# Two running sums for the first expert stage, picks made in the routers, and earlier loads of up-weights

## The chip, the cores and the metric

One core of a Trainium2 chip runs the whole program. The time is device microseconds from start to end of one execution.

## The reference

The input is 4 x 1024 tokens of 256 features. The program is two layers; what the change touches is the mixture-of-experts block, which both have at their end:

```python
h = gelu(concat([xf, stats(xf)]) @ r1_w.T + r1_b)
probs = softmax(h @ r2_w.T)                       # 32 experts
topp, topi = top_k(probs, 2)
score = where(routed, probs, -inf)
idx = argsort(-score, axis=0)[:cap].T             # cap = 160 tokens for each expert
gate, upv = split(xf[idx] @ w_up.T, 2)            # per expert, 256 -> 2 x 512
ye = (silu(gate) * upv) @ w_down.T                # 512 -> 256
out = zeros.at[idx].add(w * ye)                   # each token is in at most two experts
```

An adapter for each pair of experts is added in the same way. Layer 0 is: x + 0.5 ffn(layernorm x), a causal attention over sums of keys, x + 0.5 ffn again, and then x + moe(layernorm x). Layer 1 is a linear attention (relu of keys and queries, `kv = k.T v` for each of the four sequences, output `q kv / (q sum k)`), added to x, and the moe block again.

## The kernel before

**Stages.** The program runs in stages with a barrier of all engines between them: the first feed-forward, attention (to 602 us), the first router `ffn_router` (to 723 us), the first `dispatch` (to 1157 us), the linear attention with the second router in it, `linear_router` (to 1405 us), and the second `dispatch` (to the end). Rows of the input lie in 32 tiles of 128 tokens, four tiles to a group; a batch is one sequence, two groups. Every engine has its own instruction list, written out by hand in a function of each stage (`sync` for SP's DMA queue, `gpsimd` for POOL, `tensor` for PE, `scalar` for ACT, `vector` for DVE); they meet in semaphores only. `Chain.link` makes DVE wait for its own last operation.

**Routers.** `RouterFront` normalizes each group, makes statistics of a row, and brings the logits of 32 experts for each token into `m.prob`; `take` on ACT is its last step. `ffn_router` has the feed-forward around it. Its first step is `layernorm_var` on DVE for all 32 tiles, the power -0.5 on POOL (`rstd_of`, line 112), and `shift` on DVE (line 1890); then ACT normalizes group by group.

**Dispatch** is `route` and then `experts`, in one block. In `route` DVE finds for each token its two best experts (`pick1`, `pick2`, lines 2055 to 2068), the sum of exponentials, and scores; then `Choice` searches, over 15 rounds, the score from which an expert's 160 tokens are taken, for the first 16 experts at once (`counts`, `decide`; `beside(k)` puts other DVE work into round k), makes lists of tokens, and POOL gathers the first rows. The second half's search runs beside the first experts. `values` on POOL runs beside the first rounds. Up to line 2073 these are operations over 32 tiles x 32 experts, 1024 values in each of 128 partitions.

**Experts** are done in quads of four, eight quads; a turn is two quads. PE's order, of one expert: five products up (the last is the adapter's), the down products of the expert before, and so on; weights lie in four buffers, and SP loads the next expert's after the down product that used the buffer has ended (`turn` in `sync`, `load_expert`), the adapters with every second expert:

```python
sp.wait_ge(full[u_down[n].bank], down[n])
m.load_expert(sp, t * 2 * EQ + n + EQ, n % EQ)     # 1 MB w_up, 0.5 MB w_down
if n % 2:
    m.load_adapter(sp, t * EQ + n // 2 + EQ // 2, n % EQ // 2)
```

A quad's 4 x 160 results are five tiles: one of 128 for each expert, and the four tails of 32 in the fifth. ACT weighs them into `y` (line 2370), and POOL adds them to the rows of x in DRAM (`add`, line 2237, an indirect DMA that adds). Within one such DMA, or between two that are under way together, no row may come twice. A token may be in two experts of a quad, but then once as its first choice and once as its second; so each quad is added in two phases of five tiles, the first choices and, once these have landed, the second. A next quad waits for both. Only in the last quad two tiles go whole, one after the other (`ALONE`): each has one expert's tokens.

**Linear stage.** SP loads x back from the sum (`x_sum`), eight groups of 512 KB, with 1.2 MB of weights behind the second. DVE makes statistics of a batch (`stats`, line 87), `norm` writes the normalized rows, PE turns them, makes keys and values tile by tile (`kv`), and sums their products; for each tile DVE writes `k_row` (line 2636), for which the sum waits. DVE's `stats(b + 2)` stands at a batch's end, ahead of the next batch's first `k_row`.

## Time and profile before

| | |
|---|---|
| median of 3 runs | 1841.35 us (1838.83 to 1843.05) |
| the profiled execution | 1842.41 us, its span 1840.7 us |
| busy: PE, DVE, ACT, POOL | 1513.0, 957.9, 728.7, 561.4 us |
| mean granted clock of PE | 0.901 of full speed |
| moved by DMA | 212.10 MB, mean 115 GB/s |

Times in the rows are microseconds from the span's start. PE is busy for 82% of the span, but not evenly: in both dispatches there is a stretch before the experts in which it waits for the search, and one behind them in which only POOL's adds run.

### The profile page before, as it was taken

What the parts mean: (1) busy time and instruction counts of PE and PEld (TensorE: products, weight loads), DVE (VectorE), ACT (ScalarE), POOL (GpSimd) and SP (SyncE); (2) the same over time, 40 slices, a digit from 0 to 9 for tenths busy, and PEclk for the clock granted to TensorE, in tenths of its full rate; (3) what the DMA queues carried; (4) which work ended last, traced back from release to release, by engine and by line L of the source; (5) the groups of instructions that cost most, each with busy time, mean ns of one, the idle gap of its engine ahead of it and who ended that gap; (6) DMA issues with size and microseconds to landing.
All of it is one profiled execution on the core that took longest, in us unless ns stands there. A gap on an engine that the chain in (4) does not pass through costs nothing. (4 is left out here: it accounts for less than half of the span.)

```text
span 1840.7 us, 26894 instructions
## 1 busy us (share of the span) xinstructions
PE 1513.0 (82%) x9512; PEld 1155.9 (63%) x9512; DVE 957.9 (52%) x2637; ACT 728.7 (40%) x1773; POOL 561.4 (30%) x465
## 2 busy tenths in 40 slices
PE   6899989999998595549999996589983559998994
PEld 5556544555554463439889896355552549888994
DVE  8766677888773495754521111366555754421120
ACT  4222157666665484415323232123332425322331
POOL 6422300000001441231637345222101231545445
PEclk9989989999999797559999998799995569999997
DMA  3033462333200133125869785411014026789774
GB/s 101 27 124 117 123 116 54 77 58 75 51 25 2 35 110 139 54 43 168 237 205 240 222 224 86 125 39 42 24 60 175 6 46 203 215 234 245 226 213 46
DMA packets 113492, 212.10 MB, mean 115 GB/s; under 512 B 20085, under 2 KB 79386, under 8 KB 104154
## 3 DMA queue, kind: packets, MB, share of 16 engines
q1 hardware_dynamic: 87066, 178.93, 30.6%
q0 software_dynamic: 26304, 31.60, 11.4%
q8 instruction: 69, 1.13, 0.3%
q14 instruction: 53, 0.43, 0.1%
HBM read 158.71 MB, written 51.38 MB: 114 GB/s over the span
## 5 line engine op out<-in xcount | busy, mean ns | idle before, releaser
L952 DVE TENSOR_REDUCE attnm_top<-psum 128x1 f32<-128x384 f32 (+3 forms) x384 | 212.8, 597 | 56.4 <-PE psum L1037 52.3
L1174 ACT ACTIVATE attnm_prob<-psum 128x512 f32<-128x512 f32 (+1 forms) x384 | 192.1, 530 | 88.3 <-PE psum L1047 81.6
L2237 POOL DMA_INDIRECT out<-moe2e_y,moe_scatter_i x76 | 119.2, 1568 | 146.6 <-ACT moe2e_y L2370 77.7
L2292 PE MATMUL psum<-moe1e_xgT,moe_w_up 128*128 128x160 f32 x1024 | 154.7, 307 | 8.6 <-issue 6.1
L2292 PE MATMUL psum<-moe2e_xgT,moe_w_up 128*128 128x160 f32 x1024 | 153.6, 305 | 9.6 <-issue 7.2
L2415 DVE SCALAR_TENSOR_TENSOR moe2e_h<-moe2e_gate,psum 128x160 f32<-128x160 f32 x160 | 50.4, 320 | 212.6 <-ACT moe2e_gate L2344 212.4
L2415 DVE SCALAR_TENSOR_TENSOR moe1e_h<-moe1e_gate,psum 128x160 f32<-128x160 f32 x160 | 50.6, 321 | 212.2 <-ACT moe1e_gate L2344 212.0
L2237 POOL DMA_INDIRECT x_sum<-moe1e_y,moe_scatter_i x76 | 119.4, 1571 | 136.6 <-ACT moe1e_y L2370 80.3
L2292 PEld LDWEIGHTS psum<-moe1e_xgT,moe_w_up 128*128 128x128 f32 x1024 | 145.9, 195 | 11.8 <-issue 11.8
L2292 PEld LDWEIGHTS psum<-moe2e_xgT,moe_w_up 128*128 128x128 f32 x1024 | 145.0, 194 | 12.7 <-issue 12.7
L1344 POOL DMA_INDIRECT moe_xg<-xn_rows,moe_gather_i x80 | 83.6, 1045 | 163.6 <-DVE moe_gather_i L1528 101.9
L938 POOL TENSOR_TENSOR attnm_tail_v<-attnm_v_tail,attnm_tail_p 128x256 f32<-128x256 f32 x32 | 19.8, 620 | 343.5 <-PE psum L1089 284.5
L1035 PE MATMUL psum<-attn_mask_ts,ident_bf 128*128 128x128 bf16 x512 | 105.9, 226 | 9.6 <-DVE attnm_top L952 7.6
L1037 PE MATMUL psum<-attnm_k_hat,attnm_q_hat 96*128 96x512 bf16 (+3 forms) x384 | 106.9, 306 | 0.0
L1047 PE MATMUL psum<-attnm_q_hat,attnm_k_hat 99*128 99x512 bf16 (+1 forms) x288 | 98.4, 345 | 1.4 <-ACT attnm_prob L1174 0.6
L2344 ACT ACTIVATE moe1e_gate<-psum 128x160 f32<-128x160 f32 x160 | 47.4, 301 | 112.1 <-PE psum L2292 111.8
L2344 ACT ACTIVATE moe2e_gate<-psum 128x160 f32<-128x160 f32 x160 | 47.2, 300 | 112.5 <-PE psum L2292 112.2
L2304 PE MATMUL psum<-moe2e_h,moe_w_down 128*128 128x160 f32 x512 | 80.4, 300 | 2.0 <-ACT moe2e_yT L2352 2.0
L2304 PE MATMUL psum<-moe1e_h,moe_w_down 128*128 128x160 f32 x512 | 80.4, 300 | 2.0 <-ACT moe1e_yT L2352 2.0
L1035 PEld LDWEIGHTS psum<-attn_mask_ts,ident_bf 128*128 128x128 bf16 x512 | 50.5, 100 | 48.3 <-issue 24.3
L1060 PE MATMUL psum<-attnm_prob,attn_v_aug 128*32 128x512 f32 (+1 forms) x768 | 78.7, 527 | 0.0
L2304 PEld LDWEIGHTS psum<-moe2e_h,moe_w_down 128*128 128x128 f32 x512 | 72.9, 190 | 2.8 <-ACT moe2e_yT L2352 2.8
(426 smaller groups left out, 3234.6 us busy)
## 6 DMA issues: line engine op xcount, KB each, us to landing
moe_w_up<-in_expert_up SPq DMA_DIRECT2D x64, 1024.0 KB, 5.5
moe_w_down<-in_expert_down SPq DMA_DIRECT2D x64, 512.0 KB, 7.2
attnm_q_hat<-q_parts SPq DMA_DIRECT2D x72, 128.0 KB, 4.6
moe_a_up<-in_adapter_up SPq DMA_DIRECT2D x32, 256.0 KB, 6.6
q_parts<-attnf_q_part SPq DMA_DIRECT2D x12, 512.0 KB, 2.8
attnm_k_hat<-k_parts SPq DMA_DIRECT2D x72, 64.0 KB, 2.3
x_res<-in_x SPq DMA_DIRECT2D x8, 512.0 KB, 8.7
v_tails<-attnf_v_tail SPq DMA_DIRECT2D x4, 1024.0 KB, 4.3
```

The source lines that it names most:

```text
L952: nc.vector.tensor_reduce(top[:, n // QUADS % 2, tiles[0]:tiles[-1] + 1, hh:hh + 1], s.ps[:, u.bank, 0:len(tiles) * width].rearrange("p (t ...
L1035: nc.tensor.matmul(out[:, width - P:width], s.identb[:], o.mask_ts[:, tile % 2, :], start=(i == 0), stop=False, skip_group_check=True)
L1037: ins = nc.tensor.matmul(out, q_hat[r][0:MROW, h, tile * P:(tile + 1) * P], k_hat[r][0:MROW, h, 0:width], start=False, stop=True, skip_gro ...
L1047: nc.tensor.matmul(s.ps[:, u.bank, at:GROUP], k_hat[r][0:MROW + NPART, h, j * P:(j + 1) * P], q_hat[r][0:MROW + NPART, h, g * GROUP + at:( ...
L1060: ins = nc.tensor.matmul(s.ps[32 * h:32 * h + 32, u.bank, at:GROUP], o.v_aug[:, first:first + 32], prob[:, i % NPROB, at:GROUP], start=(j ...
L1174: nc.scalar.activation(prob[:, i % NPROB, at:GROUP], s.ps[:, u.bank, at:GROUP], ACT.Exp).then_inc(taken[u.bank], 1)
L1344: pool.indirect_dma_start(self.xg[:, q, k, :], None, self.rows, bass.IndirectOffsetOnAxis(ap=self.gather_i[:, at:at + 1], axis=0), bounds_ ...
L2237: nc.gpsimd.indirect_dma_start(total, bass.IndirectOffsetOnAxis(ap=rows, axis=0), y[:, q, k, :], None, bounds_check=TOKENS + SPARE - 1, oo ...
L2292: ins = nc.tensor.matmul(s.ps[:, u.bank, half * CAP:(half + 1) * CAP], lhsT, xgT[:, q, c, k * CAP:(k + 1) * CAP], start=(c == 0), stop=(c ...
L2304: ins = nc.tensor.matmul(s.ps[:, u.bank, o * CAP:(o + 1) * CAP], lhsT, h[:, n % 2, i, :], start=(i == 0), stop=(i == PAIRS - 1))
L2344: nc.scalar.activation(gate[:, i, :], s.ps[:, u.bank, 0:CAP], ACT.Silu).then_inc(silu, 1)
L2415: nc.vector.scalar_tensor_tensor(out=h[:, n % 2, i, :], in0=gate[:, i, :], scalar=1.0 if i < INTER // P else SCALE_A, in1=s.ps[:, u.bank, ...
```

## The change

It has four parts.

- **Two sums.** In the first dispatch the results are added to two tensors in turn, `x_sum` and a new `x_more`, which `ffn_router` fills with zeros. Of a quad the four tiles of 128 are added whole, the fifth as first and as second choices: six adds, three to each sum. An add waits for the one before it in the same sum (`add_apart`). The linear stage loads both and adds them (`fetch`).
- **Picks beside the logits.** The picks of 24 of the 32 tiles are made in the routers (`Picks`, eleven steps), 16 tiles and then 8; `route` does the last 8 tiles. Its last two wide operations are split by half of the experts. The buffers `key` and `col` lie in the last expert's down-weights and the last adapter's buffer, so these are loaded later.
- **Up-weights early.** `load_up` goes out when the up products that used the buffer have ended, `load_down` and the adapters as before.
- **Variances in parts.** `ffn_router` takes the first 8 tiles, then 24; the linear stage's first batch is split into its two groups.

The second dispatch keeps its ten adds a quad; its route and its loads change as in the first.

```diff
+        self.key = self.w_down[EQ - 1][:].rearrange("p i c -> p (i c)").rearrange("p (t e) -> p t e", e=EXPERTS)
+        self.col = self.a_down[EQ // 2 - 1][:, 0:7 * TILES].rearrange("p (i t) -> p i t", t=TILES)
...
+class Picks:
+    STEPS = 11
+    def step(self, n, made=None):
...
+        if n == 0:
+            ins = nc.vector.tensor_reduce(top, prob, AX_X, ALU.max)
+        elif n == 1:
+            ins = nc.vector.tensor_tensor(key, prob, per_expert(top), ALU.subtract)
...
+        else:
+            ins = nc.vector.tensor_tensor(pick2, pick2, per_expert(k1), ALU.is_equal)
...
+PICKED = slice(0, TILES - 2 * GT)
...
@@ ffn_router @@
+    PARTLY = slice(0, 2 * GT), slice(2 * GT, TILES)
...
             for g in range(GROUPS):
                 r.store(sp, g)
+                sp.dma_start(more_view[g], nothing[:]).then_inc(m.more_cleared, 16)
...
-            pool.wait_ge(all_var, 1)
-            rstd_of(nc, s).then_inc(all_rstd, 1)
+            for n, part in enumerate(PARTLY):
+                pool.wait_ge(all_var, n + 1)
+                nc.gpsimd.tensor_tensor(s.rstd[:, part], s.veps[:, part], s.mhalf[:, part], ALU.pow).then_inc(all_rstd, 1)
+            nc.gpsimd.memset(nothing[:], 0.0).then_inc(nothing_made, 1)
...
+            for tiles, last in ((slice(0, 4 * GT), 3), (slice(4 * GT, PICKED.stop), GROUPS - 3)):
+                picks = Picks(nc, s, m, chain, tiles)
+                v.wait_ge(taken[r.u_l[last].bank], r.u_l[last].after(0))
+                for n in range(Picks.STEPS):
+                    picks.step(n)
...
@@ route @@
+            m.load_up(sp, k, k)
+            if k == EQ - 1:
+                sp.wait_ge(second.scored, PT)
+            m.load_down(sp, k, k)
...
+        picks = Picks(nc, s, m, chain, rest)
+        for n in range(Picks.STEPS):
+            picks.step(n, m.picked if n + 1 == Picks.STEPS else None)
         v.wait_ge(exped, 1)
+        nc.vector.tensor_reduce(total[:, done], prob[:, done], AX_X, ALU.add)
...
+        missed(first)
+        shares(first)
         first.scores(v, key, prob)
         def beside(k):
-            if 5 <= k < 5 + PT:
+            if k == 3:
+                missed(second)
+            elif k == 4:
+                shares(second)
+            elif 5 <= k < 5 + PT:
                 second.scores(v, key, prob, [k - 5])
...
@@ experts @@
+                    sp.wait_ge(full[u_up[n, INTER // P - 1].bank], up[n])
+                    m.load_up(sp, t * 2 * EQ + n + EQ, n % EQ)
                     sp.wait_ge(full[u_down[n].bank], down[n])
-                    m.load_expert(sp, t * 2 * EQ + n + EQ, n % EQ)
+                    m.load_down(sp, t * 2 * EQ + n + EQ, n % EQ)
...
+        def add_apart(quad):
+            q, t, of = quad % 2, quad // 2, m.choices[quad // late.quads]
+            first, second = (scatter_i[:, (quad * 2 + i) * ST_TILES + EQ:(quad * 2 + i) * ST_TILES + EQ + 1] for i in range(2))
+            steps = [(k, of.whole[:, quad % late.quads, k:k + 1]) for k in range(EQ)] + [(EQ, first), (EQ, second)]
+            for n, (k, rows) in enumerate(steps):
+                at, landed = (total, sum_in) if n % 2 == 0 else (m.more, more_in)
+                if quad + n // 2 > 0:
+                    pool.wait_ge(landed, 16 * (ADDS * quad + n // 2))
+                if n == 1 and quad > 0:
+                    pool.sem_inc(y_free[1 - q], 1)
+                pool.wait_ge(taken[u_y[q, k // 2].bank], u_y[q, k // 2].after(t))
+                nc.gpsimd.indirect_dma_start(at, bass.IndirectOffsetOnAxis(ap=rows, axis=0), y[:, q, k, :], None,
...
+                                             compute_op=ALU.add).then_inc(landed, 16)
...
@@ linear_router @@
+    PARTS_OF_VAR = [(0, 1), (1, 2)] + [(BG * b, BG * b + BG) for b in range(1, BATCH)]
...
+            def load_more(g):
+                if g >= MORE:
+                    sp.wait_ge(summed, g - MORE + 1)
+                sp.dma_start(more[:, g % MORE], more_view[g]).then_inc(more_in[g], 16)
...
+            for g in range(MORE, GROUPS):
+                load_more(g)
...
+            def fetch(g):
+                v.wait_ge(x_in[g], 16)
+                v.wait_ge(more_in[g], 16)
+                xg = s.x[:, GT * g:GT * g + GT, :]
+                nc.vector.tensor_tensor(xg, xg, more[:, g % MORE], ALU.add).then_inc(summed, 1)
...
                 if b + 2 < BATCH:
-                    stats(b + 2)
+                    fetch(BG * (b + 2))
+                    fetch(BG * (b + 2) + 1)
+                    stats(b + 3)
```

**SP in the experts' turn.** The piece is the first two experts of the third turn; `bank5` holds the down products and `bank0` to `bank3` the up products. Before:

```order
L1350 DMA moe_w_up<-in_expert_up 128x2048 [waits moe1e_bank5_full]
L1351 DMA moe_w_down<-in_expert_down 128x1024
L1350 DMA moe_w_up<-in_expert_up 128x2048 [waits moe1e_bank5_full]
L1351 DMA moe_w_down<-in_expert_down 128x1024
L1355 DMA moe_a_up<-in_adapter_up 128x512
L1356 DMA moe_a_down<-in_adapter_down 128x256
```

In the changed program:

```order
L1355 DMA moe_w_up<-in_expert_up 128x2048 [waits moe1e_bank3_full]
L1358 DMA moe_w_down<-in_expert_down 128x1024 [waits moe1e_bank5_full]
L1355 DMA moe_w_up<-in_expert_up 128x2048 [waits moe1e_bank0_full]
L1358 DMA moe_w_down<-in_expert_down 128x1024 [waits moe1e_bank5_full]
L1362 DMA moe_a_up<-in_adapter_up 128x512
L1363 DMA moe_a_down<-in_adapter_down 128x256
```

The loads keep their order; each `moe_w_up` now waits for an up product instead of a down product, so that it goes out behind the `moe_w_down` of the expert before, and the adapter's two loads have only a `moe_w_down` directly ahead of them.

**POOL at the end of the first experts.** `x_sum` and `x_more` are the two sums, `c_whole` the rows of a whole tile, `scatter_i` those of one choice. Before:

```order
L1344 DMA moe_xg<-xn_rows,moe_gather_i 128x272 x5
L2237 DMA x_sum<-moe1e_y,moe_scatter_i 4736x256 x10
L1344 DMA moe_xg<-xn_rows,moe_gather_i 128x272 x5
L2237 DMA x_sum<-moe1e_y,moe_scatter_i 4736x256 x20
L2237 DMA x_sum<-moe1e_y,moe_c_whole 4736x256 x2
L2237 DMA x_sum<-moe1e_y,moe_scatter_i 4736x256 x6
```

In the changed program:

```order
L2345 DMA x_sum<-moe1e_y,moe_c_whole 4736x256
L2345 DMA x_more<-moe1e_y,moe_c_whole 4736x256
L2345 DMA x_sum<-moe1e_y,moe_c_whole 4736x256
L2345 DMA x_more<-moe1e_y,moe_c_whole 4736x256
L2345 DMA x_sum<-moe1e_y,moe_scatter_i 4736x256
L2345 DMA x_more<-moe1e_y,moe_scatter_i 4736x256
```

Of the last quad, six adds stand where eight stood, and of each quad before it six where ten stood, to alternating targets.

**SP at the start of the linear stage.** `lin_more` is the buffer of two groups for the second sum. Before:

```order
L2578 DMA x_res<-x_sum 128x4x256 x2
L2580 DMA lin_w<-in_lin_wqkv 128x2x768
L2581 DMA lin_w<-in_lin_wout 128x2x256
L2582 DMA lin_bias<-in_lin_bout 128x256
L2578 DMA x_res<-x_sum 128x4x256 x6
```

In the changed program:

```order
L2704 DMA x_res<-x_sum 128x4x256
L2701 DMA lin_more<-x_more 128x4x256
L2704 DMA x_res<-x_sum 128x4x256
L2701 DMA lin_more<-x_more 128x4x256
L2708 DMA lin_w<-in_lin_wqkv 128x2x768
L2709 DMA lin_w<-in_lin_wout 128x2x256
L2710 DMA lin_bias<-in_lin_bout 128x256
L2704 DMA x_res<-x_sum 128x4x256 x6
L2701 DMA lin_more<-x_more 128x4x256 x6
```

Two groups of the second sum are loaded right behind the same groups of x, the other six behind all of x.

## Rows read from the trace of the kernel before

**Rows 1.** Windows: stretch, us, busy us of each engine, granted clock, DMA share, GB/s.

```profile
1206.00:1405.00 199.00, 173.91 (x654) 106.34 (x652) 108.85 (x378) 71.56 (x175) 36.49 (x21) 0.95 0.13 43
...
1662.00:1743.00 81.00, 73.49 (x520) 71.84 (x520) 13.42 (x44) 22.85 (x73) 41.05 (x30) 0.96 0.81 223
```

**Rows 2.** Timeline (start us, us, engine, line, op): first router's start.

```profile
605.02 5.46 POOL L112 TENSOR_TENSOR rstd<-var_eps,minus_half 128x32 f32<-128x32 f32 x1 [8.81 <-DVE var_eps L107]
610.51 0.19 DVE L1890 SCALAR_TENSOR_TENSOR ffn_shift<-mean,rstd 128x32 f32<-128x32 f32 x1 [5.57 <-POOL rstd L112]
```

**Rows 3.** Timeline, linear stage: reciprocal root for eight tiles on POOL.

```profile
1166.36 1.68 POOL L2592 TENSOR_TENSOR rstd<-var_eps,minus_half 128x8 f32<-128x8 f32 x1 [8.89 <-DVE var_eps L2627]
```

**Rows 4.** Timeline: first router's last row, first dispatch's first row on DVE.

```profile
722.35 0.27 ACT L1773 COPY moe_prob<-psum 128x128 f32<-128x128 f32 x1 [0.63 <-PE psum L1808]
...
723.63 0.06 DVE L2054 MEMSET moe1e_zero<- 128x1 f32 x1 [13.54 <-PEq L58]
```

**Rows 5.** Timeline, DVE, first dispatch: route's picks and scores.

```profile
724.89 1.22 DVE L2056 TENSOR_TENSOR moe1e_y<-moe_prob,moe1e_y 128x1024 f32<-128x1024 f32 x1
...
741.38 0.90 DVE L1406 SCALAR_TENSOR_TENSOR moe_c_above<-moe1e_y,moe_prob 128x128 f32<-128x128 f32 x4
...
752.84 0.16 DVE L1449 TENSOR_SCALAR_CACHE_REDUCE moe_c_passed<-psum 128x3 f32<-128x3 f32 x1 [0.17 <-PE psum L1600]
...
763.86 0.69 DVE L1424 TENSOR_TENSOR moe_c_score<-moe_c_score,moe_c_equal 128x512 f32<-128x512 f32 x1
```

**Rows 6.** Timeline, DVE beside POOL in the linear stage's start.

```profile
1173.40 2.06 DVE L95 TENSOR_TENSOR mean<-x_stats 128x8 f32<-128x8 f32 x1
...
1176.30 0.42 DVE L2636 TENSOR_SCALAR lin_k_row<-psum 128x256 f32<-128x256 f32 x1
```

**Rows 7.** Waits of PE in the first experts: us in total, times, longest us.

```profile
PE psum L2292 <- issue: 6.1, 2, 3.8
```

**Rows 8.** The same in the second experts.

```profile
PE psum L2292 <- issue: 7.2, 4, 4.6
```

**Rows 9.** Timeline, PE, second experts.

```profile
1664.38 4.61 PE L2292 MATMUL psum<-moe2e_xgT,moe_w_up 128*128 128x160 f32 x32 [0.54 <-ACT moe2e_xgT L2360]
...
1700.72 6.88 PE L2292 MATMUL psum<-moe2e_xgT,moe_w_up 128*128 128x160 f32 x32 [4.58 <-issue]
```

**Rows 10.** Timeline, SP, second experts: the adapter's lower weights, issued before that gap.

```profile
1689.34 0.65 SPq L1356 DMA_DIRECT2D moe_a_down<-in_adapter_down  x1
```

**Rows 11.** Tile moe_a_down, SP, 1687 to 1690 us: its one load.

```profile
DMA to landing us min/median/max: 11.0/11.0/11.0
```

**Rows 12.** Timeline, POOL: the last adds of the first dispatch.

```profile
1106.83 1.55 POOL L2237 DMA_INDIRECT x_sum<-moe1e_y,moe_scatter_i  x1 [19.82 <-ACT moe1e_y L2370]
...
1130.79 1.55 POOL L2237 DMA_INDIRECT x_sum<-moe1e_y,moe_c_whole  x1 [3.07 <-DMA x_sum<-moe1e_y,moe_scatter_i]
1135.34 1.55 POOL L2237 DMA_INDIRECT x_sum<-moe1e_y,moe_c_whole  x1 [3.00 <-ACT moe1e_y L2370]
...
1151.78 1.55 POOL L2237 DMA_INDIRECT x_sum<-moe1e_y,moe_scatter_i  x1 [0.30 <-issue]
```

**Rows 13.** Timeline, ACT: the last weighted tiles of the first dispatch.

```profile
1134.40 1.20 ACT L2370 ACTIVATE moe1e_y<-psum,moe1e_weight 128x256 f32<-128x256 f32 x3 [0.82 <-PE psum L2273]
```

**Rows 14.** Windows of the linear stage's start, columns as in rows 1.

```profile
1162.00:1164.00 2.00, 0.00 (x0) 0.00 (x0) 1.66 (x5) 0.00 (x0) 0.00 (x0) 0.50 1.08 383
...
1174.00:1178.00 4.00, 3.86 (x12) 1.91 (x11) 3.04 (x10) 0.74 (x2) 2.97 (x2) 1.00 0.55 177
```

**Rows 15.** Timeline, DVE: first statistics of the linear stage.

```profile
1162.22 2.93 DVE L87 BATCH_NORM_STATS2 x_stats<-x_res 128x6 f32<-128x256 f32 x8 [34.74 <-DMA x_res<-x_sum]
```

**Rows 16.** Timeline: from the first batch to the second of the linear stage.

```profile
1217.62 2.70 DVE L87 BATCH_NORM_STATS2 x_stats<-x_res 128x6 f32<-128x256 f32 x8
...
1221.38 0.42 DVE L2636 TENSOR_SCALAR lin_k_row<-psum 128x256 f32<-128x256 f32 x1
...
1221.86 1.13 PE L2743 MATMUL psum<-lin_v_row,lin_k_row 128*128 128x257 f32 x4 [3.12 <-DVE lin_k_row L2636]
```

208 lines of the change are left out of this document (140 added, 68 removed).

## The prediction

> **What bounds the kernel now.** I read the windows first: one row per stage, to see which engine fills it. In the second half of the program PE does: 73.5 of 81 us in a turn of the second experts, 173.9 of 199 us in most of the linear stage [rows 1]. So only those parts of the change can pay that touch a place where PE stands still. The view of waits and the timeline around each stage's edge then show five such places, and the change touches all of them.
>
> **1. Start of the first router.** Before anything is normalized POOL raises 32 columns to the power -0.5 in 5.46 us, and DVE's shift comes at 610.51 [rows 2]; ACT, PE and all the rest wait for it. The change does eight columns first. Eight columns take 1.68 us [rows 3]. DVE's chain of eight short operations ahead is about as long for 8 columns as for 32, so the shift comes 5.46 - 1.68 = 3.8 us sooner. The other 24 columns (by the line through these two rows 0.16 us a column and 0.4 fixed, 4.2 us) end some 5.9 us after DVE's first part, at about 611, and are first used by the third group's normalization, several microseconds later; the memset of 128x1024 zeros behind them on POOL (about 1 us) delays the first bias add, which DVE needs only after PE's first product. I take **-3.9** (with a little for the shorter DVE operations), bounds -3.5 and -4.2. The eight extra writes of 512 KB of zeros go out from SP between stores that wait for DVE anyway; nobody waits for that queue until the stage's end: nothing.
>
> **2. End of the first router.** DVE is done 13.54 us before the next stage's first row at 723.63, so at 710.1; the last copy of probabilities ends at 722.62 [rows 4]. Into this gap go both sets of picks: 11 steps over 16 tiles (512 values) and 11 over 8 tiles (256). An operation takes 1.22 us over 1024 values, 0.69 over 512 [rows 5], 0.42 over 256 [rows 6], and each step waits for the one before, some 0.03 us more. That is 11 x 0.72 + 11 x 0.45 = 12.9 us: DVE ends at 723.0, 0.4 us after ACT. **+0.5**, bounds 0 and +1.5. In the linear stage the same 22 steps cost almost nothing: those over 16 tiles stand in the last batch's gaps of DVE behind each k_row (I allow +0.4, since one stands ahead of the queries), those over 8 tiles at the end, where PE still has the last two logits to make.
>
> **3. Start of both dispatches.** Until the first scores are out only DVE works: 723.63 to 742.28, 18.65 us [rows 4, 5]. After the change: 11 steps over 256 values (5.0), the sum of 768 (about 0.95 by the line) and of 256 (0.45), reciprocal (0.4), two operations over 512 instead of 1024 (1.4), the scores (0.90): 9.1 us, with ACT's exponentials beside them. That gives -9.5. Back comes the second half's share of the last two operations, put into search rounds 3 and 4: 2 x 0.69 us, where DVE's idle time in a round is 0.17 [rows 5], so +1.0 if nothing else happens. POOL works beside them. DVE's operation of two inputs beside a long POOL operation took 2.06 us instead of some 0.2 [rows 6]; if each of the two meets that, it is +4. I take +1.3, nearer the low end, because the row at the high end stands beside a POOL operation over 2048 values, and POOL's here are over 512. So **-8.2** each, **-16.4** for both, bounds -10 and -17.4. The page "GPSIMD Engine Reference" of the Trainium skill (section 1, Specifications) says that GpSimd shares its SBUF interfaces with VectorE and that instructions with two SBUF inputs contend; by it each of the two added operations can be held, and the pair of dispatches would give about 5 us less. The 2.06 us row agrees; no row shows such an operation of 512 values held.
>
> **4. Weights in the experts.** PE idles ahead of the up-products for a total of 6.1 us in the first experts and 7.2 in the second [rows 7, 8]. The longest, 4.58 us, ends at 1700.72 [rows 9]; the adapter's lower weights were issued at 1689.34 and landed 11.0 us later, at 1700.3 [rows 10, 11]. So "issue" there is a late adapter: it stands in SP's queue behind 1 MB of up-weights and 0.5 MB of down-weights that are issued in the same moment. After this gap PE runs 32 matmuls in 6.88 us against 4.61 [rows 9], as at a lower granted clock: +2.3. In the first experts I reckon 1.7 for the same. Sum 6.1 + 7.2 + 2.3 + 1.7 = 17.3. After the change the up-weights go out one expert earlier, and the adapter stands behind 0.5 MB only. At the rate of 1.9 MB in 11 us, 1 MB less is -5.8 us for it; at the highest rate seen, 383 GB/s [rows 14], -2.7. The adapter is then on time or up to 1.9 us late. I take **-15.5**, bounds -8 and -17.3. In the first experts there are also fewer adds (48 against 76) on the same DMA engines. SP's new waits are on products that end before the ones it waited for already; nothing is queued behind them but the weights themselves.
>
> **5. The adds at the end of the first experts.** An add of 128 rows takes POOL 1.86 us to issue, and the one that must wait for it starts 4.55 us after it (1130.79 to 1135.34) [rows 12]. Before: ten adds of quad 6 from 1106.83, then quad 7's eight in four steps; the last is issued at 1151.78 and lands about 1156.3. After: quad 6 needs three links of 4.55 in each sum, side by side, and is in by 1122.4. Quad 7's tiles 0 and 1 follow at about 1123.6, tiles 2 and 3 once ACT has weighed them (from 1134.40, done with tile 3 at about 1135.1 [rows 13]), tile 4 twice at 1139.7 and 1141.5. The last lands at 1146.1: **-10.2**, bounds -9 and -11. This is the tail's price; the second experts keep the old adds and their tail.
>
> **6. The join in the linear stage.** DVE now adds 512 KB blocks of the second sum, and they have to be loaded. The first statistics wait for x until 1162.22 [rows 15]; all 5.4 MB of loads were through at about 1176, at up to 383 GB/s [rows 14]. SP puts the third and fourth blocks of the second sum behind all eight of x, and DVE must add both before its first k_row. That is 4 x 0.52 = 2.1 MB more, at 370 GB/s 5.7 us: the fourth is in at 1181.7, its add (1.22 [rows 5]) ends at 1183.1. From the start of the statistics over two groups to k_row it is 1221.38 - 1217.62 = 3.8 us [rows 16]. So the first k_row starts at 1186.9 instead of 1176.30 [rows 6]: +10.6. PE, which has two key products done, waits for it; the granted clock was 1.00 in 1174 to 1178 [rows 14] and falls, +2 more (0 to 4). From batch to batch DVE is late already: PE waits 3.12 us for k_row behind the statistics [rows 16]. Two more adds stand there in two of the batches: 4 x 1.25 = +5.0. With the 0.4 above: **+18.0**, bounds +10 and +23.
>
> **Sum:** -3.9 + 0.5 - 16.4 - 15.5 - 10.2 + 18.0 = -27.5. The profiled execution took 1842.4 us (span 1840.7), 1 us more than the median of the runs, 1841.35. That makes 1814.9 for it and 1813.9 for the median: I say **1814**. A difference of 0.2%, 3.7 us, is about what a measurement can tell from none.
>
> **The rivals.**
> A. *The adapter stays late*, because gathers and adds, not the up-weights, fill the DMA engines there: part 4 gives nothing, 1829. For it: DMA is busy for 0.81 of that turn [rows 1]. Against: the 1.5 MB ahead of it are, even at 383 GB/s, 4 of its 11 us. Chance 0.12.
> B. *The join waits for no load*: the blocks come as early as DVE can take them. Then the head costs DVE's own work, two adds, the split statistics and two more, about 5 us: 1814 - 7.6 = 1806. For it: rates of 383 GB/s are not the ceiling for certain. Chance 0.13.
> C. *The two sums don't overlap*: each add waits for the one before it, whichever sum it goes to. Six links of 4.55 are 27.3 us: quad 6 is in at 1134.1, quad 7 at 1161.4, 5 us later than before: 1829. The change would not do what it says. Against: each sum has a semaphore of its own. Chance 0.05.
> D. *POOL and DVE hold each other* in the search rounds at the 2.06 us price: 1819. Chance 0.05.
> E. *Slower: the clock stays low.* PE loses its upper level in the wait for the join and does not get it back for a batch. A batch is some 48 us of PE work (173.9 in about 3.6 batches [rows 1]), so 48 us more: 1860. It decides from about 31 us of such work. Against: after 34.74 us in which even DVE had waited for the first rows [rows 15] the granted clock was 1.00 by 1174 [rows 14]. Chance 0.03. The page "TensorE: Matmul & The Clock Gate" (the Trainium skill, "Seeing it yourself") reports a gate held low for over 50 us; no row here shows that.
>
> My forecast has the remaining 0.62.
>
> **How the numbers follow.** A to D lie between 1806 and 1829 and only E is slower than before. The terms' own bounds, not all at one end, add 11 to either side. The range is 1803 to 1829; what it leaves out is E and the ends of A, B and C, less than 2 in 10. Faster 0.95, same 0.01, slower 0.04 (E, and a sum of upper bounds).
>
> **What would show it.** Right: the first router's shift near 606.7; 9 to 10 us from a dispatch's start to its scores; no PE gap over 1 us ahead of an up-product; add pairs 4.55 us apart, the linear stage starting some 12 us after ACT's last weighted tile instead of 22; and DVE waiting for the block of the second sum until some 24 us after the linear stage's start. Wrong: an adapter that still lands after PE wants it, adds spaced 4.5 us one by one, PE's clock low through the first batch, or a k_row that comes within 3 us of its old distance from the stage's start.

## The result, and the profile after

The changed kernel takes **1815.67 us** (median of 4 runs, 1813.92 to 1820.00) against 1841.78 for the kernel before: a ratio of 0.9864, 95% interval 0.9842 to 0.9886. The forecast was 1814, range 1803 to 1829. The profiled execution took 1817.1 us, its span is 1815.4.

From the page of the changed kernel: busy time of each engine, and two rows of the 40 slices (45.4 us each).

```profile
PE 1512.8 (83%) x9512; PEld 1152.6 (63%) x9512; DVE 975.4 (54%) x2716; ACT 730.0 (40%) x1775; POOL 517.4 (28%) x438
...
PE   6899979999998677549999996588995549999994
...
PEclk9989989999999898559999998799996559999997
```

PE's busy time is what it was (1513.0 us before); what went is time in which it stood still. The 26th slice (1135 to 1180 us; 5 in the row of PE, 7 in that of its clock) is the start of the linear stage, where the join stands.

To see which term moved, I cut both executions at the same landmarks: first row of the router on DVE, first row of a dispatch, first up-product of its experts, ACT's last weighted tile, SP's first load of the linear stage, first row of the second dispatch, first up-product, end. All in us; "attention" is everything up to the first router, which the change does not touch.

| | attention | router | dispatch 1 | experts 1 | tail | first k_row | linear | dispatch 2 | experts 2 |
|---|---|---|---|---|---|---|---|---|---|
| before | 603.6 | 120.0 | 95.0 | 315.8 | 23.9 | 18.0 | 247.9 | 94.8 | 339.7 |
| changed | 606.9 | 117.0 | 85.7 | 309.5 | 14.6 | 29.0 | 265.9 | 85.7 | 330.1 |

("tail" runs from the last weighted tile to the first load; "first k_row" is counted from the first load and is part of "linear".) The differences are +3.2, -2.9, -9.3, -6.3, -9.3, linear +18.0, -9.1, -9.6: -25.3, the difference of the spans. So 46.5 us were won at six places, 18.0 given back in one, and 3.2 are the attention part, where the two programs are the same: scatter.

First router, DVE, timeline (start us, us, engine, line, op), answering to [rows 2]:

```profile
606.88 0.17 DVE L95 TENSOR_TENSOR mean<-x_stats 128x8 f32<-128x8 f32 x1 [1.35 <-PEq L58]
...
609.74 0.19 DVE L1958 SCALAR_TENSOR_TENSOR ffn_shift<-mean,rstd 128x8 f32<-128x8 f32 x1 [0.63 <-POOL rstd L1927]
613.87 0.18 DVE L1958 SCALAR_TENSOR_TENSOR ffn_shift<-mean,rstd 128x24 f32<-128x24 f32 x1 [3.94 <-POOL rstd L1927]
```

The shift that the first normalization waits for comes 2.9 us after the stage's first row, where it took 6.9. The one for the other 24 columns comes 4.1 us later, and nobody waits for it.

First dispatch, DVE, and two rows of POOL:

```profile
723.92 0.06 DVE L2139 MEMSET moe1e_zero<- 128x1 f32 x1 [2.14 <-PEq L58]
...
728.89 0.42 DVE L1866 TENSOR_TENSOR moe_pick<-moe_pick,moe_a_down 128x256 f32<-128x256 f32 x1
729.23 0.94 DVE L2144 TENSOR_REDUCE moe_a_down<-moe_prob 128x24 f32<-128x768 f32 x1
...
732.25 0.90 DVE L1413 SCALAR_TENSOR_TENSOR moe_c_above<-moe_w_down,moe_prob 128x128 f32<-128x128 f32 x4
...
745.03 1.05 POOL L1561 TENSOR_TENSOR moe_value<-moe_pick,tile_no 128x512 bf16<-128x512 f32 x1
745.30 0.81 DVE L1450 TENSOR_SCALAR moe_c_ahead<-tries_no,moe_c_tries 128x4 f32<-128x4 f32 x1
...
746.02 0.68 DVE L2132 SCALAR_TENSOR_TENSOR moe_w_down<-moe_pick 128x512 f32<-128x512 f32 x1
746.06 2.07 POOL L1563 TENSOR_SCALAR moe_value<-moe_pick,row_no 128x512 bf16<-128x512 f32 x1
...
748.51 0.69 DVE L2136 TENSOR_TENSOR moe_prob<-moe_prob,moe_a_down 128x512 f32<-128x512 f32 x1
```

Eleven picks over 256 values end at 729.3, where the old ones over 1024 went on to 737.4; the scores start 8.3 us into the stage instead of 17.8 [rows 5]. The rows of 0.68 and 0.69 us are the second half's two operations in search rounds 3 and 4. Neither was held, but neither met an operation of POOL that was already under way: the first began just as POOL's operation of two inputs ended (746.08), and POOL's next took 2.07 us where it takes 1.56 in other rounds; the second (748.51) began after POOL's last (748.13). What POOL did hold is the small operation ahead of them, 4 values wide, 0.81 us instead of 0.23; that was so before the change too. These rounds took 3.08 and 2.54 us, the same two before 2.57 and 2.45.

First experts, the waits of PE (us in total, times, longest). No wait ahead of an up-product over 1 us is left there (6.1 us before, [rows 7]), nor in the second experts; the longest is 0.7 us. What is left in the first experts stands ahead of down-products (L2421) and of y's transposes (L2389):

```profile
PE psum L2389 <- ACT moe1e_yT L2469: 3.4, 3, 2.1
PE psum L2421 <- issue: 3.0, 3, 1.8
```

The last adds of the first experts on POOL [rows 12], and ACT's last weighted tiles:

```profile
1108.93 1.55 POOL L2345 DMA_INDIRECT x_sum<-moe1e_y,moe_c_whole  x1 [4.44 <-ACT moe1e_y L2487]
1110.78 1.55 POOL L2345 DMA_INDIRECT x_more<-moe1e_y,moe_c_whole  x1 [0.30 <-issue]
1120.78 1.55 POOL L2345 DMA_INDIRECT x_sum<-moe1e_y,moe_c_whole  x1 [8.44 <-ACT moe1e_y L2487]
1122.64 1.55 POOL L2345 DMA_INDIRECT x_more<-moe1e_y,moe_c_whole  x1 [0.30 <-issue]
1125.22 1.55 POOL L2345 DMA_INDIRECT x_sum<-moe1e_y,moe_scatter_i  x1 [1.03 <-DMA x_sum<-moe1e_y,moe_c_whole]
1127.08 1.55 POOL L2345 DMA_INDIRECT x_more<-moe1e_y,moe_scatter_i  x1 [0.30 <-issue]
```

```profile
1119.12 1.20 ACT L2487 ACTIVATE moe1e_y<-psum,moe1e_weight 128x256 f32<-128x256 f32 x3 [0.82 <-PE psum L2389]
```

The two sums do overlap: an add to one is issued 1.85 us after an add to the other, and 4.4 us after the one of its own sum that it must wait for (1120.78 to 1125.22, 1122.64 to 1127.08).

Start of the linear stage, all engines, from SP's first load to the first k_row [rows 6, 15]:

```profile
1133.68 0.38 SPq L2704 DMA_DIRECT2D x_res<-x_sum  x1
...
1139.04 1.22 DVE L2755 TENSOR_TENSOR x_res<-x_res,lin_more 128x1024 f32<-128x1024 f32 x1 [26.85 <-DMA lin_more<-x_more]
...
1151.31 4.51 POOL L2727 TENSOR_TENSOR x_res<-x_res,lin_bias 128x2048 f32<-128x2048 f32 x1 [1.57 <-DVE lin_xn L118]
...
1156.49 2.52 DVE L2755 TENSOR_TENSOR x_res<-x_res,lin_more 128x1024 f32<-128x1024 f32 x2 [5.33 <-DMA lin_more<-x_more]
...
1162.66 0.76 DVE L2775 TENSOR_SCALAR lin_k_row<-psum 128x256 f32<-128x256 f32 x2
```

DVE waits 5.33 us for the third block of the second sum; the first k_row starts 29.0 us after the first load (18.0 before). PE waits for k_rows in the whole stage:

```profile
PE psum L2900 <- DVE lin_k_row L2775: 14.6, 5, 5.4
```

The longest three are 5.01 us at the first k_row, 5.41 at the second batch's start and 3.11 at the third's; before they were nothing, 3.12 [rows 16] and 0.83. The batch starts stand +11.0, +14.8, +18.6 and +18.6 us later, counted from the first load.

### The profile page after: what moved, and what is told of

Its sections match the earlier page's. It is cut to its first block and busy times, and to the rows that moved or that the text cites. A ratio compares the mean times of both kernels' runs of the same rounds, so it can differ in the third digit from the quotient of the medians.

```text
span 1815.4 us, 26993 instructions
## 1 busy us (share of the span) xinstructions
PE 1512.8 (83%) x9512; PEld 1152.6 (63%) x9512; DVE 975.4 (54%) x2716; ACT 730.0 (40%) x1775; POOL 517.4 (28%) x438
## 5 line engine op out<-in xcount | busy, mean ns | idle before, releaser
L2421 PE MATMUL psum<-moe1e_h,moe_w_down 128*128 128x160 f32 x512 | 80.3, 300 | 3.6 <-issue 3.0
L2421 PE MATMUL psum<-moe2e_h,moe_w_down 128*128 128x160 f32 x512 | 80.3, 300 | 2.1 <-ACT moe2e_yT L2469 1.2
L2421 PEld LDWEIGHTS psum<-moe1e_h,moe_w_down 128*128 128x128 f32 x512 | 72.9, 190 | 4.3 <-issue 3.5
L1045 PE MATMUL psum<-attn_mask_st,ident_bf 128*128 128x256 bf16 x256 | 70.4, 277 | 5.4 <-DMA attn_q_first<-attnm_mT 5.3
```

The costliest lines, as they stand in the source:

```text
L2421: ins = nc.tensor.matmul(s.ps[:, u.bank, o * CAP:(o + 1) * CAP], lhsT, h[:, n % 2, i, :], start=(i == 0), stop=(i == PAIRS - 1))
```

## The experiments

Eleven kernels ran, on three chips. The ratios are to the kernel before on the same chip, with the 95% interval; its median there was 1841.5, 1839.1 and 1838.3 us, and the changed kernel was measured apart from them, beside 1841.8. So where a time is set against the changed kernel's 1815.67, up to 3 us can be the chip's. First the same table, from their profiled executions; each experiment is read in the stages that it touches, because the others scatter (attention: 598.9 to 606.9).

| | attention | router | dispatch 1 | experts 1 | tail | first k_row | linear | dispatch 2 | experts 2 |
|---|---|---|---|---|---|---|---|---|---|
| one_sum | 601.5 | 116.5 | 85.8 | 307.9 | 23.9 | 19.6 | 247.9 | 85.5 | 331.4 |
| one_by_one | 604.2 | 116.3 | 85.7 | 317.8 | 32.1 | 20.1 | 249.9 | 85.6 | 330.4 |
| blocks_early | 600.1 | 117.4 | 85.7 | 308.2 | 14.6 | 27.7 | 263.5 | 86.0 | 329.4 |
| blocks_early_bias_late | 601.5 | 116.9 | 85.8 | 306.5 | 14.5 | 23.4 | 258.7 | 85.6 | 329.8 |
| gaps | 606.5 | 117.3 | 85.6 | 306.6 | 14.9 | 22.8 | 245.3 | 86.0 | 330.9 |
| one_sum_gaps | 601.7 | 116.5 | 85.7 | 308.0 | 23.8 | 19.1 | 243.9 | 85.6 | 329.7 |
| up_late | 600.8 | 117.1 | 85.9 | 315.6 | 14.6 | 29.3 | 266.2 | 85.6 | 334.9 |
| up_late_one_wait | 601.0 | 116.8 | 85.7 | 319.8 | 14.8 | 29.4 | 266.0 | 85.7 | 335.8 |
| before_adapter_first | 601.7 | 119.9 | 94.7 | 307.5 | 24.0 | 18.0 | 247.0 | 94.4 | 330.6 |
| gaps_adapter_ahead | 605.0 | 117.4 | 85.8 | 316.3 | 14.6 | 23.1 | 248.7 | 85.7 | 329.6 |
| picks_late | 598.9 | 120.2 | 95.3 | 317.1 | 14.8 | 29.5 | 265.9 | 95.2 | 330.8 |

### What the second sum costs and brings: one_sum, one_by_one

one_sum:

```diff
-        self.more = s.x_more if out is None else None
+        self.more = None
...
-                nc.vector.tensor_tensor(xg, xg, more[:, g % MORE], ALU.add).then_inc(summed, 1)
```

(and neither the zeros nor the loads of the second sum).

> The changed kernel without the second sum: the adds of the first experts as they were before (half tiles in phases), no zeros written, no blocks of a second sum loaded or added in the linear stage; everything else as changed. My theory (terms 5 and 6 of the prediction, as the two traces bear them out: the stretch from ACT's last weighted tile to SP's first load fell from 23.9 to 14.6 us, the linear stage grew from 247.9 to 265.9): +9.3 and -18.0, so 8.7 us faster than the changed kernel, about 1807. Rival 1, the fewer adds (48 instead of 76) are what took PE's stalls out of the first experts: these come back, +6, about 1813. Rival 2, the linear stage's growth is not the join but something else of the change: no gain there, about 1825.

Measured: 1804.28 us, 0.9807 (0.9762 to 0.9851), 11.4 us under the changed kernel. Tail 23.9, linear stage 247.9, both to the tenth what they were before the change, and the first experts kept their gain (307.9). So the second sum, by itself, loses 8.7 us: 9.3 won in the tail, 18.0 paid in the linear stage. The first k_row comes at 19.6 us, 1.6 later than before the change: that is the split statistics alone. Rival 1 (fewer adds relieve PE) and rival 2 fall.

one_by_one keeps whole tiles, without the second sum:

```diff
-                at, landed = (total, sum_in) if n % 2 == 0 else (m.more, more_in)
-                if quad + n // 2 > 0:
-                    pool.wait_ge(landed, 16 * (ADDS * quad + n // 2))
+                at, landed = total, sum_in
+                if quad + n > 0:
+                    pool.wait_ge(landed, 16 * (2 * ADDS * quad + n))
```

> one_sum, but with the tiles added whole, each add waiting for the one before: what the first experts' adds of the changed kernel would be without the second sum. My theory (a link is 4.55 us, and two sums halve their number): the last quad's six adds stand in one chain behind the six of the quad before; from the quad's first add at 1091.6 in the changed kernel's time 12 links of 4.55, so SP's first load of the linear stage 29 us after ACT's last weighted tile, against 23.9 with half tiles and 14.6 with two sums: 1809 to 1810. Rival (the adds' own spacing, not the order, sets the end): 15 to 20 us, 1797 to 1800.

Measured: 1821.71 us, 0.9903 (0.9874 to 0.9932): 17 us over one_sum, where I had said 5. The tail is 32.1 us, not 29. POOL's adds:

```profile
1087.05 1.55 POOL L2341 DMA_INDIRECT x_sum<-moe1e_y,moe_scatter_i  x1 [8.60 <-DMA x_sum<-moe1e_y,moe_c_whole]
1093.74 1.55 POOL L2341 DMA_INDIRECT x_sum<-moe1e_y,moe_scatter_i  x1 [5.14 <-DMA x_sum<-moe1e_y,moe_scatter_i]
1099.17 1.55 POOL L2341 DMA_INDIRECT x_sum<-moe1e_y,moe_c_whole  x1 [3.88 <-DMA x_sum<-moe1e_y,moe_scatter_i]
...
1149.42 1.55 POOL L2341 DMA_INDIRECT x_sum<-moe1e_y,moe_scatter_i  x1 [2.98 <-DMA x_sum<-moe1e_y,moe_scatter_i]
```

Quad 5's last links, under the loads of weights, are 6.7 and 5.4 us long, so quad 6's chain (from 1099.17) starts 2.7 us later against the end than I had counted it; from there the links are 4.6 us on the average. The chain is the price of whole tiles: 32.1, 23.9 with half tiles in phases, 14.6 with two sums.

Another 9.9 us stand in the first experts (317.8 against 307.9), and I had not counted them. The chain makes them too. The gathers of quad 7's rows stand in POOL's list behind quad 4's adds; they were issued at 1052.82 to 1058.21, and PE waited for them, in this kernel alone:

```profile
PE psum L2372 <- DMA moe_xg<-xn_rows,moe_gather_i: 7.4, 3, 5.1
```

```profile
1063.99 1.12 PE L2372 MATMUL psum<-ident,moe_xg 128*128 128x128 f32 x4 [5.11 <-DMA moe_xg<-xn_rows,moe_gather_i]
```

In the changed kernel the last of them was issued at 1039.17 and wanted at 1062.0. Behind the wait PE's granted clock was 0.50 (1064 to 1070 us), and its work in the stage took 2.8 us more than in one_sum. Together that is the stage's loss; it and the tail's 8.2 us account for the 17 us. So two sums are also worth what a single chain costs ahead of the tail.

### Where the join's 18 us stand: blocks_early, blocks_early_bias_late, gaps, one_sum_gaps

blocks_early, in SP's queue:

```diff
             for g in range(GROUPS):
...
+                if g == 3:
+                    load_more(2)
+                    load_more(3)
-            for g in range(MORE, GROUPS):
+            for g in range(4, GROUPS):
```

> The changed kernel with one thing moved: SP issues the third and fourth block of the second sum behind x's fourth group instead of behind all eight. My theory (the head of the linear stage waits for these loads, which stand behind 2.1 MB of x): DVE's second pair of adds no longer waits for a load, the first k_row comes at 23 to 24 us after SP's first load instead of 29.0, and the kernel is about 5 us faster than the changed one, 1810 to 1811. Rival, the head is bound by DVE's own work or by PE's products: the k_row stays within 1 us of 29.0, 1815 to 1816.

Measured: 1810.78 us, 0.9841 (0.9797 to 0.9885). The time is near my figure, but the step that should have made it is not: the first k_row came at 27.7, not at 23 to 24, and the linear stage is only 2.4 us shorter. The rest of the 4.9 us stands in parts that the edit does not touch. Timeline, all engines:

```profile
1143.45 6.67 DVE L2758 TENSOR_TENSOR x_res<-x_res,lin_more 128x1024 f32<-128x1024 f32 x2
...
1143.66 5.38 POOL L2730 TENSOR_TENSOR x_res<-x_res,lin_bias 128x2048 f32<-128x2048 f32 x1 [1.57 <-DVE lin_xn L118]
...
1153.79 0.76 DVE L2778 TENSOR_SCALAR lin_k_row<-psum 128x256 f32<-128x256 f32 x2
```

The tile lin_more on DVE (duration in ns: min/median/max):

```profile
L2758 DVE TENSOR_TENSOR x_res<-x_res,lin_more x8: 1217/1224/5329, 1131.4 to 1255.0; 128x1024 f32<-128x1024 f32 x8
```

DVE no longer waits for a load. But of its two adds one took 5.33 us instead of 1.22. It lies beside POOL's addition of the bias to 2048 elements, itself 5.38 us instead of 4.51. One bound went and the next stood 1.3 us behind it. The page "GPSIMD Engine Reference" of the Trainium skill (section 1, Specifications) says that GpSimd contends with VectorE's instructions that have two SBUF inputs, and the 5.33 us agree. I had used that rule in part 3, where neither added operation was held, and not here.

blocks_early_bias_late, on POOL:

```diff
+            rstd(2)
             pool.wait_ge(w_in, 48)
             add_bias(0)
-            rstd(2)
```

> blocks_early, and on POOL the bias added to the first batch behind the third power instead of ahead of it. In blocks_early DVE's wait for the third block was gone, but one of its two adds took 5.33 us instead of 1.22, beside POOL's addition of the bias (5.38 us instead of 4.51, two inputs as well). My theory: DVE's operation of two inputs stands still while POOL's runs. Then both adds take 1.22 each here, the first k_row comes at 23.6 us after SP's first load (27.7 in blocks_early, 29.0 in the changed kernel), and the linear stage is 4 us shorter than in blocks_early. Rival: the add was slow because the loads were still filling the buffers beside it; it takes 5.3 again and the k_row stays at 27 to 28.

Measured: 1803.35 us, 0.9813 (0.9778 to 0.9847). First k_row 23.4, linear stage 258.7, 4.8 us shorter than in blocks_early. All eight adds:

```profile
L2758 DVE TENSOR_TENSOR x_res<-x_res,lin_more x8: 1218/1224/1227, 1130.5 to 1249.4; 128x1024 f32<-128x1024 f32 x8
```

So it was POOL's operation and not the loads. The head of the join is now DVE's own work: two more adds and the split statistics, 5.4 us over the kernel before, 1.6 of which one_sum has without any adds.

gaps, on top of blocks_early (DVE):

```diff
             norm(0, 1)
-            fetch(2)
-            fetch(3)
-            stats(2)
...
                     keys(b, k)
+                    if b == 0:
+                        for job in {1: [(fetch, 2)], 2: [(fetch, 3)], 3: [(stats, 2)]}.get(k, []):
+                            job[0](job[1])
+                    for job in {(0, 4): [(fetch, 4)], (0, 5): [(fetch, 5)], (0, 6): [(stats, 3)],
+                                (1, 3): [(fetch, 6)], (1, 5): [(fetch, 7)], (1, 6): [(stats, 4)]}.get((b, k), []):
+                        job[0](job[1])
```

(the same pieces are gone from the ends of the batches).

> blocks_early, and DVE's adds and statistics of the next batches no longer ahead of the first k_row or at a batch's end, but one piece at a time behind the k_rows of the batch before, where DVE idles some 2 us each time. My theory (the join costs only where DVE is waited for): first k_row at about 23 us after SP's first load (the first products end there), no wait of PE for k_row at the batches' starts (5.0 and 5.4 us in the changed kernel, 3.1 in the kernel before), a linear stage of about 247 us against 265.9, 1796 to 1799 in all. Rival: what DVE does in the gaps delays the k_rows one for one; the stage stays above 258 us, 1808 or more.

Measured: **1795.47 us**, 0.9766 (0.9733 to 0.9799), 20 us under the changed kernel. First k_row 22.8, linear stage 245.3: shorter than before the change, with the whole join in it. PE's waits for k_rows, 14.6 us in the changed kernel:

```profile
PE psum L2902 <- DVE lin_k_row L2778: 2.8, 3, 1.6
```

one_sum_gaps has the same edit on top of one_sum.

> one_sum (1804.3), with the statistics of the next batches in the same gaps. My theory: PE's waits of 3.1 us at two batches' starts go, and the head gets 1 to 2 us shorter: a linear stage of about 240 us against 247.9, 1796 to 1797. Rival (the statistics at the batches' ends lie beside work of PE that bounds there anyway): 1803 to 1805.

Measured: 1795.81 us, 0.9776 (0.9736 to 0.9817). Linear stage 243.9 instead of 247.9, half of what I expected (that the median hit my figure is luck): the head won 0.5 us, the second batch's start 1.5 and the third's 2.0 (64.7 to 62.7 and 119.9 to 115.9 us from the first load). By the stages the second sum is now worth 9.0 - 1.4 = 7.6 us (tail 14.9 against 23.8), but the medians of the two are 0.3 us apart: the profiled executions differ by 4.9 in the attention part, the other way. That it wins is shown for these two stages, not for the whole.

### What the early up-weights do: up_late, before_adapter_first, up_late_one_wait, gaps_adapter_ahead

up_late, SP in the experts:

```diff
-                    sp.wait_ge(full[u_up[n, INTER // P - 1].bank], up[n])
-                    m.load_up(sp, t * 2 * EQ + n + EQ, n % EQ)
                     sp.wait_ge(full[u_down[n].bank], down[n])
+                    m.load_up(sp, t * 2 * EQ + n + EQ, n % EQ)
```

> The changed kernel with each expert's up-weights issued again at the end of its down-product, ahead of the down-weights, as before the change. My theory (term 4: the adapter stands behind 1.5 MB in SP's queue): PE's gaps ahead of the up-products are back in both experts' stages, +13 to +16, about 1830. Rival A' (the gain of the first experts came from their fewer adds): only the second experts lose, +9.6, about 1825. Rival A (early up-weights do nothing): 1816.

Measured: 1823.75 us, 0.9916 (0.9891 to 0.9942). First experts +6.1, second experts +4.8. Rival A falls; of my 13 to 16 us 10.9 came back. But of the gaps that my theory names even less did: PE stood ahead of up-products 2.4 us in the first experts (one gap) and 4.5 in the second, where the kernel before has 6.1 and 7.2. The first experts' waits there:

```profile
PE psum L2420 <- issue: 4.2, 3, 1.7
PE psum L2407 <- issue: 2.4, 1, 2.4
```

The one ahead of up-products (L2407) stands where the kernel before has its first (some 140 us into the stage), so rival A' falls too. The waits ahead of down-products (L2420) were 3.0 us in the changed kernel, and PE's own work in the stage took 3.1 us more than there (297.7 against 294.6), at a lower granted clock, of which the last section has more.

before_adapter_first moves one thing in the kernel before:

```diff
-                    m.load_expert(sp, t * 2 * EQ + n + EQ, n % EQ)
                     if n % 2:
                         m.load_adapter(sp, t * EQ + n // 2 + EQ // 2, n % EQ // 2)
+                    m.load_expert(sp, t * 2 * EQ + n + EQ, n % EQ)
```

> The kernel before with one thing moved: where an adapter pair is due, SP issues it ahead of the 1.5 MB of up- and down-weights instead of behind them; all are issued in the same moment as before. If the gaps are a matter of the order in the queue (my theory), they go here too, although nothing is issued earlier: the adapter, issued at 1688.9 and wanted at 1696.6, lands in about 5 us, and the kernel takes 1841.8 less 12 to 16, 1826 to 1830. If what helped was the earlier issue of the up-weights themselves (rival: the DMA engines are full there, and the up-weights would now be late in the adapter's place), the gaps stay: 1840 to 1842.

Measured: 1823.13 us, 0.9904 (0.9876 to 0.9932). First experts 307.5, second 330.6: the whole gain of part 4 (8.3 and 9.1 us) by the order in the queue, with nothing issued earlier.

up_late_one_wait adds to up_late:

```diff
                 pe.wait_ge(up_in[k], 32 * t + 16 * q + 16)
+                pe.wait_ge(down_in[k], 32 * t + 16 * q + 16)
```

> up_late, and an up-product waits for its expert's down-weights too, as in the kernel before, where one semaphore counted both. up_late gave back 6.1 us in the first experts and only 4.8 of 9.6 in the second. If the other half of the gain was that an up-product need not wait for down-weights (theory W), PE's gaps ahead of up-products return in full and the second experts take 339 to 340 us (334.9 in up_late), the kernel 1828 to 1830. If it was scatter of the transfers from one execution to the next (theory S), the stage stays at 334 to 336 and the kernel within 2 us of up_late's 1823.8.

Measured: 1827.17 us, 0.9940 (0.9907 to 0.9973). Second experts 335.8, where theory W wanted 339 to 340. The waits of PE there:

```profile
PE psum L2408 <- DMA moe_a_down<-in_adapter_down: 5.1, 3, 2.7
```

The transfer named is the adapter's. For the second experts' time theory S holds, though 5.1 us of gaps ahead of up-products are there; why up_late's order gave 335 there and the kernel before 339.7 stays open, and one profile of each cannot tell it from scatter. The kernel's time, 3.4 us over up_late's, lies in neither theory's range. Most of that is the first experts (319.8 against 315.6), where PE waits 6.2 us ahead of down-products.

gaps_adapter_ahead, on top of gaps:

```diff
-                    m.load_down(sp, t * 2 * EQ + n + EQ, n % EQ)
                     if n % 2:
                         m.load_adapter(sp, t * EQ + n // 2 + EQ // 2, n % EQ // 2)
+                    m.load_down(sp, t * 2 * EQ + n + EQ, n % EQ)
```

> gaps (1795.5), and an adapter pair is issued ahead of the down-weights of the same moment. In the changed kernel PE still stands 3.0 us ahead of down-products and 1.2 to 3.4 us behind late copies of ACT in each experts' stage, nowhere ahead of an up-product. Theory: the adapter is early enough already, so nothing to gain: within 2 us of 1795.5. Rival (the adapter is at the edge, and some executions lose 2 to 4 us on it): 1792 to 1793 and less scatter.

Measured: 1803.27 us, 0.9779 (0.9735 to 0.9823), with runs from 1794.9 to 1805.6: inconclusive. It brings no gain, and its profile differs from that of gaps in the first experts (316.3 against 306.6). One wait stands where the edit bears, ahead of the products with the down-weights that now go out behind the adapter:

```profile
884.39 1.99 PE L2421 MATMUL psum<-moe1e_h,moe_w_down 128*128 128x160 f32 x8 [3.05 <-issue]
```

The same place took 0.28 us in gaps, but 1.77 in the changed kernel, whose order is that of gaps. So that the edit costs something is likely, and not shown. PE's own work took 4.4 us more than in gaps (299.0 against 294.6), by the clock, as the last section shows.

### Parts 1 to 3 undone: picks_late

```diff
-            for tiles, last in ((slice(0, 4 * GT), 3), (slice(4 * GT, PICKED.stop), GROUPS - 3)):
...
-        key, col, done, rest = m.key, m.col, PICKED, slice(PICKED.stop, TILES)
+        key, col, rest = m.key, m.col, slice(0, TILES)
...
-    PARTLY = slice(0, 2 * GT), slice(2 * GT, TILES)
+    PARTLY = (slice(0, TILES),)
```

> The changed kernel with parts 1 to 3 undone: no picks in the routers' last stretches (all eleven steps over all 32 tiles stand in the dispatch again, with the exponential behind them), and one power over 32 columns. My theory: the head of a dispatch is longer by 11 steps of 1.25 instead of 0.46 us (+8.8) and by 0.6 us more of exponential and sum, so the scores start 17.8 us into the stage instead of 8.35, and each first up-product comes 9.4 us later; the first router is 3 to 4 us longer by the power (117.0 to about 120), since the picks at its end cost nothing; the linear stage is the same within 0.5 us. +21, 1837. Rival (the picks cost the routers some of what they save the dispatches): the first router comes out at 119 or less, and the linear stage is more than 1 us shorter.

Parts 1 to 3 are those of the prediction; the second sum, the early up-weights and the linear stage's split statistics stay.

Measured: 1841.40 us, 1.0015 (0.9993 to 1.0037). DVE at the first dispatch's start:

```profile
719.10 0.06 DVE L2133 MEMSET moe1e_zero<- 128x1 f32 x1 [13.57 <-PEq L58]
719.10 1.22 DVE L1846 TENSOR_REDUCE moe_a_down<-moe_prob 128x32 f32<-128x1024 f32 x1
...
731.68 1.23 DVE L1866 TENSOR_TENSOR moe_pick<-moe_pick,moe_a_down 128x1024 f32<-128x1024 f32 x1
734.03 1.22 DVE L2139 TENSOR_REDUCE moe_a_down<-moe_prob 128x32 f32<-128x1024 f32 x1 [1.12 <-ACT moe_prob L2094]
...
737.00 0.90 DVE L1413 SCALAR_TENSOR_TENSOR moe_c_above<-moe_w_down,moe_prob 128x128 f32<-128x128 f32 x4
```

The scores start 17.9 us into the stage (17.8 expected), both dispatches are 9.6 and 9.5 us longer, the router is 120.2, the linear stage 265.9, the same to the tenth. So the 22 steps in the routers' ends cost next to nothing (point 2 below has the rest): the rival falls. The kernel came out 4 us over my 1837; the profile has that, and more, in the first experts (317.1), which this edit does not touch, and the shortest attention part of all (598.9) the other way. Whether its first experts take 317 in every run, one profile does not show.

## Why the prediction was right, point by point

**1, the router's start: -3.9, measured -4.0** (shift at 2.86 instead of 6.87 us).

**2, the router's end: +0.5, measured nothing in the changed kernel and +0.6 in three others.** In the changed kernel DVE was done with the picks at 721.8, 1.1 us before ACT's last copy. But that copy was late by PE's clock. The products of the last group but one, in the changed kernel and in one_sum:

```profile
709.42 3.41 PE L1806 MATMUL psum<-ffn_r_xnT,r 128*128 128x512 f32 x4 [3.58 <-ACT ffn_r_statT L1766]
```

```profile
704.39 1.96 PE L1806 MATMUL psum<-ffn_r_xnT,r 128*128 128x512 f32 x4 [3.58 <-ACT ffn_r_statT L1766]
```

The granted clock was 0.56 during the first. That is 1.45 us, and it is why router and start together give only -2.9 in that profile. In one_sum, one_by_one and up_late these products ran at the upper level; there DVE's last pick ended 0.3 us after ACT's last copy, as I had worked out (0.4), and the stage ended 0.6 us later than that copy alone would have let it. Why the clock was low there in the changed kernel and five of the experiments, no run shows. In the linear stage the +0.4 did not come.

**3, the dispatches: -8.2 each, measured -9.3 and -9.1.** The sum for the head was right (-9.4 at the scores). The term mis-sized was what is given back: +1.3, measured +0.6 in the rounds, of which 0.5 was regained by the first up-product. I had taken the idle time of one round (0.17) for all. That round is one in which POOL holds DVE's small operation for 0.6 us; in the rounds behind POOL's last operation DVE idles 0.56 to 0.75 us, and the second operation all but disappeared there (+0.1). That neither was held came of where they fell, not of their 512 values: a hold beside POOL's operations of 512 is in the traces, before and after. picks_late gave all of it back.

**4, the weights: -15.5, measured -6.3 - 9.6 = -15.9.** The cause was the one named, an adapter behind 1.5 MB in SP's queue: before_adapter_first wins the same by order alone. That the up-weights go out one product earlier is one way to shorten that queue, and not needed for itself. The sum without my allowance for a late rest was 17.3, and before_adapter_first won 17.4. What stays open is why up_late gave back only 10.9.

**5, the adds' tail: -10.2, measured -9.3** (24 us to 14.6). The links were 4.4 to 4.5 us and the pairs 1.85 apart, as read. What I had short is the first add of quad 7's third tile: issued 1.7 us after ACT began to weigh the last tiles (1119.12 to 1120.78), where I had counted 0.7.

**6, the join: +18.0, measured +18.0**, and that it is the same to the tenth is luck: the parts are right to about a microsecond each, and their errors cancel. Head +10.6 (+11.0); PE's waits at two batches' starts +5.0 (+4.6: 3.12 to 5.41 and 0.83 to 3.11); clock +2 (+3.1, for it fell twice, to 0.62 in 1162 to 1166 us and, behind the wait of 5.41, to 0.50 in 1212 to 1216, where it had been 1.00 before; the second fall was not in my sum); the early steps +0.4 (the stage's end gave 0.6 back). And the working of the head was only half of it. It priced one bound, the loads, and rival B said that without it the head would cost 5 us. blocks_early shows a second one 1.3 us behind, POOL's addition of the bias, in which DVE's add of two inputs stands still. Rival B's 1806 would have been about 1811; its 5 us came only once the bias was moved too (5.4).

Rivals A, C, D and E did not happen: no gap ahead of an up-product; adds in pairs; neither of the two added operations held in the search rounds; and PE's clock, at its lower level (1.2 GHz) for a moment after the wait, back: the granted clock was 0.62 in 1162 to 1166 us and 0.96 in 1166 to 1170.

Outside all terms, the attention part took 3.2 us more than in the profile of before, by scatter. Without it the profiled spans would be 28.5 us apart, against 27.5 forecast; the medians are 26.1 apart. That the forecast of 1814 was met within 2 us is in part luck: parts 1 and 2 together came out 0.5 us worse than forecast, part 3 2.0 better, part 4 0.4 better, part 5 0.9 worse, and the attention part added 3.2.

## What to carry to other kernels

A second sum, or any split whose halves must be joined, should be priced in the stage that joins, and the join placed where the joining engine idles: with its adds ahead of the first k_row and at the batches' ends it cost twice what it brought (18.0 against 9.3 us), in the gaps between k_rows 1.4 (245.3 against 243.9), by the stages; the times of the whole, 1795.5 and 1795.8, do not show the gain. A chain that is not split costs in two places, at its end and in whatever the same engine has to issue behind it. Ask of a late transfer what stands ahead of it in its queue, before issuing anything earlier. And when a wait is taken away, look which other engine works beside the instruction that waited: the next bound may stand a microsecond behind.
